# A transformer block's cross attention: scores turned so that the keys lie on the partitions, and the softmax of one sequence moved beside the projections of the next

## The reference, cut to what matters

```python
q = (layernorm(x) @ Wq) ; k = context @ Wk ; v = context @ Wv        # split in 8 heads of 64
attn = softmax(einsum('bhnd,bhmd->bhnm', q, k) * 64**-0.5, axis=-1)   # n: 128 queries, m: 2048 keys
out = einsum('bhnm,bhmd->bhnd', attn, v) ; x = x + out @ Wo + bo
```

## Time and profile before

| | |
|---|---|
| median of 3 runs | 1712.08 us (1709.21 to 1714.39) |
| the profiled execution: its time, its span | 1703.06 us, 1701.1 us |
| cross attention in it (start to the last instruction at L591) | 0 to 1140.5 us |
| busy over the span: TensorE, ScalarE, VectorE, GpSimd | 96%, 39%, 38%, 32% |
| mean granted clock of TensorE | 0.99 of 2.4 GHz |

### The profile page before, as it was taken

How to read it: one execution, slowest core, us unless ns; L and a number is a source line. 1 busy time by engine, 2 the same in 40 slices (tenths; PEclk the granted TensorE clock), 3 DMA queues, 4 the chain that set the end, 5 groups by cost and what they waited for, 6 DMA issues and landing times. The chain is left out here.

```text
span 1701.1 us, 23083 instructions
## 1 busy us (share of the span) xinstructions
PE 1634.1 (96%) x9230; PEld 1290.6 (76%) x9231; DVE 648.4 (38%) x1079; ACT 663.5 (39%) x1196; POOL 541.3 (32%) x326
## 2 busy tenths in 40 slices
PE   7999999999999999999999999998889998999998
PEld 6667887887887888788788888773457686877876
DVE  6316325424523523632532542444365461222222
ACT  3225334434433533533433443342444433354421
POOL 6221132044043023124113304003620046768661
PEclk9999999999999999999999999999999998999999
DMA  5230121121111021021012112014200076656521
GB/s 209 88 99 26 39 68 50 32 74 50 32 63 46 17 81 50 26 73 59 25 32 75 50 32 81 1 36 170 75 1 1 21 259 143 172 148 188 162 56 35
DMA packets 70393, 125.15 MB, mean 74 GB/s; under 512 B 12000, under 2 KB 28448, under 8 KB 70304
## 3 DMA queue, kind: packets, MB, share of 16 engines
q1 hardware_dynamic: 40192, 92.14, 16.6%
q10 hardware_dynamic: 25296, 23.34, 4.7%
q0 software_dynamic: 4816, 8.41, 2.6%
HBM read 100.74 MB, written 24.43 MB: 74 GB/s over the span
## 5 line engine op out<-in xcount | busy, mean ns | idle before, releaser
L220 POOL TENSOR_TENSOR ctx_h<-stage,one 128x1024 fp32r<-128x1024 f32 x62 | 117.4, 1894 | 759.1 <-PE ps_t L288 759.1
L288 PE MATMUL ps_s<-ctx_h,wk 128*128 128x512 f32 x1024 | 325.4, 393 | 9.3 <-DVE ctx_l L498 9.3
L288 PE MATMUL ps_t<-wv,ctx_h 128*128 128x512 f32 x1024 | 317.7, 392 | 0.0
L542 DVE TENSOR_TENSOR kT<-ps_s,kT 64x512 fp32r<-64x512 f32 x128 | 87.5, 683 | 426.2 <-ACT kT L455 425.4
L288 PEld LDWEIGHTS ps_s<-ctx_h,wk 128*128 128x128 f32 x1024 | 193.5, 189 | 49.7 <-issue 9.9
L288 PEld LDWEIGHTS ps_t<-wv,ctx_h 128*128 128x128 f32 x1024 | 192.3, 188 | 42.3 <-issue 2.9
L564 DVE TENSOR_REDUCE smax<-ps_s 128x1 f32<-128x1024 f32 x128 | 150.6, 1218 | 142.1 <-PE ps_s L306 140.9
L288 PE MATMUL ps_s<-ctx_l,wk 128*128 128x512 f32 x512 | 200.3, 391 | 0.0
L288 PE MATMUL ps_t<-wv,ctx_l 128*128 128x512 f32 x512 | 199.3, 389 | 0.0
L438 ACT ACTIVATE probs<-ps_s,nmax 128x1024 f32<-128x1024 f32 x128 | 142.0, 1123 | 91.6 <-DVE nmax L567 91.6
L454 ACT ACTIVATE kT<-ps_s 64x512 fp32r<-64x512 f32 x128 | 75.6, 591 | 261.8 <-PE ps_s L288 168.3
(11 more groups left out here) (236 smaller groups left out, 2228.1 us busy)
## 6 DMA issues: line engine op xcount, KB each, us to landing
stage<-in_ctx_dram SPq DMA_DIRECT2D x64, 512.0 KB, 3.8
raw_u<-in_up_dram SPq DMA_DIRECT2D x32, 512.0 KB, 4.0
stage<-in_down_dram SPq DMA_DIRECT2D x16, 512.0 KB, 4.0
raw_e<-in_down_dram SPq DMA_DIRECT2D x16, 512.0 KB, 4.1
rows_scratch<-wxo SPq DMA_DIRECT2D x25, 256.0 KB, 4.6
wxo<-rows_scratch ACTq DMA_DIRECT2D x23, 256.0 KB, 3.4
q_scratch<-kT ACTq DMA_DIRECT2D x4, 1024.0 KB, 5.5
qa<-q_scratch ACTq DMA_DIRECT2D x32, 128.0 KB, 3.0
```

The lines of the kernel that those rows point to most:

```text
L220: nc.gpsimd.tensor_tensor(hi, raw, one[:, 0:1].unsqueeze(2).broadcast_to([P, 2, QT]), ALU.mult).then_inc(hi_done, 1)
L288: mm = nc.tensor.matmul(out, w(c), m(c), start=(c + k == 0), stop=(c == DC - 1 and k == 2))
L542: nc.vector.tensor_tensor(kT[XD:P, 0, p, keys], ps_s[0:XD, p, :], kT[0:XD, 0, p, keys], ALU.subtract)
```

## The change

Scores are made with the roles exchanged: a tile of 128 keys is the weight, and the queries' hi and lo parts stand side by side in one tile `q2` as 256 columns. The result has keys on the partitions, in hi and lo halves that ScalarE copies (hi) and VectorE adds (lo) into a big tile `s`. So the probabilities need no turning. But the maximum and the sum over the keys now run across the partitions. The maximum is taken over the 16 tiles on VectorE, group by group, then turned on TensorE, reduced, put on a diagonal and spread back by a matmul with ones; VectorE subtracts it from all of `s`. The sum is made by GpSimd (`tree`) and a matmul with ones. The scores of a group are made between projections, and the softmax and `values` of `b - 1` stand in the first group of `b`. `kT` holds one group, the projections share two banks `ps_p`, and the DMAs of the queries and of the output are issued by `sp`. The value projections of groups 0 and 1 come first in sequence 0.

```diff
+            def scores(b, g, h):
+                n = nth_s(b, g, h)
+                pe.wait_ge(k_lo, 2 * (nth_k(b, g, h // 2) + 1))
+                pe.wait_ge(q_in, (b + 1) * (16 * 8))
+                if n >= 2:
+                    pe.wait_ge(s_summed, n - 1)
+                for i in range(4):
+                    mm = nc.tensor.matmul(ps_ab[:, n % 2, i].rearrange("p w t -> p (w t)"),
+                                          kT[:, h % 2, h // 2, i * P:(i + 1) * P],
+                                          q2[:, h].rearrange("p w t -> p (w t)"), start=True, stop=True)
+                mm.then_inc(s_done, 1)
...
+            for b in range(1, B):                    # TensorE
+                for p in range(PAIRS):
+                    project_k(b, 0, p)
+                    if p == 0:
+                        turn_max(b - 1, 1)
+                        turn_max(b - 1, 2)
+                    if p == 1:
+                        turn_max(b - 1, 3)
+                        spread_max(b - 1, 1)
+                    if p == 2:
+                        spread_max(b - 1, 2)
+                        spread_max(b - 1, 3)
+                for t in range(4):
+                    project_v(b, 0, t)
+                for p in range(PAIRS):
+                    values(b - 1, p)
+                keys_and_scores(b, 1)
+                values_and_scores(b, 1, lambda t: sums(b - 1) if t == 1 else None)
+                for p in range(PAIRS):
+                    project_k(b, 2, p)
+                values_and_scores(b, 2)
+                last_group(b)
...
+            def key_hi(b, g, p):                     # ScalarE
+                act.wait_ge(proj_done, projected(b, "K", g, p))
+                n = nth_s(b, g, 2 * p) - XH
+                if n >= 0:
+                    act.wait_ge(s_done, n + 2)
...
+            def copy_score(b, g, h):
+                n = nth_s(b, g, h)
+                act.wait_ge(s_done, n + 1)
+                if b and g == 0:
+                    act.wait_ge(pv_done, (b - 1) * PAIRS + h // 2 + 1)
+                    act.wait_ge(sum_done, (b - 1) * XH + h + 1)
...
+                nc.scalar.activation(s[:, h, 4 * g:4 * g + 4, :], ps_ab[:, n % 2, :, 0, :], ACT.Copy).then_inc(a_copied, 1)
+            def exps(b, h):
+                act.wait_ge(shifted, b * XH + h + 1)
+                for j in range(2):
+                    part = s[:, h, 8 * j:8 * j + 8, :]
+                    nc.scalar.activation(part, part, ACT.Exp, scale=X_SCALE).then_inc(exp_done, 1)
...
+            def add_low(b, g, h):                    # VectorE
+                nc.vector.tensor_tensor(part, part, ps_ab[:, n % 2, :, 1, :], ALU.add).then_inc(s_summed, 1)
+            def max_two(b, h):                       # reduce of 1024 elements: groups 0 and 1
+                nc.vector.tensor_reduce(pm[:, h, :], s[:, h, 0:8, :].rearrange("p c t -> p t c"), AX_X, ALU.max)
...
+            def max_group(b, g, heads, count):       # reduce of 512 elements, then the merge into pm
+                    nc.vector.tensor_reduce(pmx[:, h % 2, :], s[:, h, 4 * g:4 * g + 4, :].rearrange("p c t -> p t c"),
+                                            AX_X, ALU.max).then_inc(part_max, 1)
...
+                    nc.vector.tensor_tensor(pm[:, h, :], pm[:, h, :], pmx[:, h % 2, :], ALU.max).then_inc(count, 1)
...
+            def diagonal(b, p):
+                nc.vector.tensor_reduce(mcol[:, 2 * p:2 * p + 2], max_room(p).rearrange("p (e t) -> p e t", e=2), AX_X, ...
+                nc.vector.tensor_tensor(diag[:, p % 2], ident (broadcast), mcol (broadcast), ALU.mult).then_inc(diag_done, 1)
+            def shift(b, h):
+                largest_score = max_room(h // 2)[:, h % 2 * T:(h % 2 + 1) * T].unsqueeze(1).broadcast_to([P, MT, T])
+                nc.vector.tensor_tensor(s[:, h], s[:, h], largest_score, ALU.subtract).then_inc(shifted, 1)
+            def output(b):
+                nc.vector.reciprocal(on[:, :, :].rearrange("p h t -> p (h t)"), ps_m[:, :]).then_inc(r_done, 1)
...
+            for b in range(1, B):
+                shift(b - 1, 0)
+                key_low(b, 0, 0)
+                diagonal(b - 1, 1)
+                diagonal(b - 1, 2)
+                key_low(b, 0, 1)
+                shift(b - 1, 1)
+                diagonal(b - 1, 3)
+                key_low(b, 0, 2)
+                key_low(b, 0, 3)
+                for h in range(2, XH):
+                    shift(b - 1, h)
...
+            def tree(b, h):                          # GpSimd: 3 adds of 512 elements, one of 256, one of 128
...
+            for b in range(B):
+                for k in range(4, LB):
+                    split_ctx(b, k)
+                if b < LASTB:
+                    for k in range(4):
+                        split_ctx(b + 1, k)
+                for h in range(XH if b < LASTB else XH // 2):
+                    tree(b, h)
```

More of the change, by code:

```diff
@@ L257, in turn_x, with sums @@
+            def sums(b):
+                pe.wait_ge(sum_done, (b + 1) * XH if b < LASTB else b * XH + XH // 2)
+                if b == LASTB:
+                    pe.wait_ge(late_sum, XH // 2)
+                for h in range(XH):
+                    mm = nc.tensor.matmul(ps_m[h % 2 * XD:(h % 2 + 1) * XD, h // 2 * T:(h // 2 + 1) * T], ones[:, :],
+                                          sum_room(b, h), start=True, stop=True)
+                mm.then_inc(l_done, 1)
             def turn_x(n):
@@ L399, in _, with keys_and_scores, values_and_scores @@
-            for b in range(B):
-                batch(b, b == 0)
+            def keys_and_scores(b, g, also=None):
+                for p in range(PAIRS):
+                    project_k(b, g, p)
+                    scores(b, g - 1, 2 * p)
+                    scores(b, g - 1, 2 * p + 1)
+                    if also:
+                        also(p)
+            def values_and_scores(b, g, also=None):
+                for t in range(4):
+                    scores(b, g, 2 * t)
+                    scores(b, g, 2 * t + 1)
+                    project_v(b, g, t)
+                    if also:
+                        also(t)
@@ L489, in _ @@
+            for h in range(XH):
+                exps(LASTB, h)
         @block.vector
@@ new lines, in last_group @@
+            def last_group(b):
+                for t in range(4):
+                    for h in (2 * t, 2 * t + 1):
+                        add_low(b, NQ - 1, h)
+                    max_group(b, NQ - 1, (2 * t, 2 * t + 1), pm_done)
+                    if t == 1:
+                        diagonal(b, 0)
+            statistics(0)
+            normalise(0)
+            for n in range(HB):
+                copy_xT(n)
+            statistics(1)
+            normalise(1)
+            for n in range(2):
+                query_low(n)
@@ new lines, in _ @@
+            for p in range(PAIRS):
+                key_low(0, 0, p)
+                if p < 2:
+                    query_low(p + 2)
+                else:
+                    copy_xT(2 * p)
+                    copy_xT(2 * p + 1)
+            for p in range(PAIRS):
+                key_low(0, 1, p)
+                add_low(0, 0, 2 * p)
+                add_low(0, 0, 2 * p + 1)
+                query_low(PAIRS + p)
+            for p in range(PAIRS):
+                key_low(0, 2, p)
+                add_low(0, 1, 2 * p)
+                add_low(0, 1, 2 * p + 1)
@@ new lines, in _ @@
+            shift(LASTB, 0)
+            diagonal(LASTB, 1)
+            diagonal(LASTB, 2)
+            shift(LASTB, 1)
+            diagonal(LASTB, 3)
+            for h in range(2, XH):
+                shift(LASTB, h)
+            for h in range(XH // 2, XH):
+                dve.wait_ge(exp_done, 2 * (LASTB * XH + h + 1))
+                nc.vector.tensor_reduce(sum_room(LASTB, h), s[:, h, :, :].rearrange("p c t -> p t c"), AX_X, ALU.add) \
+                    .then_inc(late_sum, 1)
+            output(LASTB)
```

688 lines of the change are left out of this document (393 added, 295 removed).

## The result

| | before | after |
|---|---|---|
| median of four runs each | 1712.15 us (1709.21 to 1714.39) | 1774.53 us (1772.0 to 1776.1) |
| ratio | 1 | 1.0364, 95% interval 1.0344 to 1.0384 |
| span of the profiled execution | 1701.1 us | 1774.3 us |
| end of cross attention in it | 1140.5 us | 1203.3 us |
| mean granted clock | 0.99 | 0.956 |

The changed kernel is 3.6% slower, 62 us. The forecast was 1685, 1.6% faster, and its range ended at 1745, so the measured time lies 30 us beyond it. In the two profiles the end of cross attention moved by 62.8 us.

The account below looks back on a forecast made before the run. TensorE, busy 96% of the span, was taken as the bound. Opening 162.4 + 7 sequences x 130.1 (119.4 work, 9.3 waits, 1.4 clock) + tail 39.6 = 1112.7 against 1140.5, giving 1685 us; range 1640 to 1745.

Parts of the forecast that it names:

- the price of the reduces: VectorE's strided reduces for the maxima, priced as dense ones: 0.69 us for 512 elements, 1.22 for 1024.
- rival B: VectorE's reduces from SBUF are also held by GpSimd: +7 us a sequence, +49, 1734 us; chance 0.14.
- Step 2 of the waits: Second group's keys and scores: a round's chain takes 4.1 us against 3.7 of content, losing 1.2 a sequence.
- Content of TensorE: TensorE's work in one sequence without waits: 119.4 us, 13.0 less than before.
- rival D: Weight loads of the score matmuls not hidden, scores at 0.2267 us each: +103 us, 1789; chance 0.07.
- First group: TensorE waits for the diagonals on VectorE, mainly before the third spreading: 5.8 us lost a sequence.
- Rival A: Holds and gap are mild, first group loses 2.8, no clock fall: 125.1 us a sequence, 1646 us; chance 0.20.
- Group 2's values and group 3: TensorE's waits for late VectorE in later stages; the fourth group was to lose 0.7 us a sequence.
- The hold of merges beside the splits: VectorE merges with two SBUF inputs wait up to 2.4 us for GpSimd's splits, on average some 1.1.
- The trees: GpSimd's sums over the keys' tiles: 5.3 us each with four gaps, ready 2 us before the copies need them.
- rival C: Late GpSimd trees delay score copies: slower than before from 6.3 us a tree, 1722 us at 6.5; chance 0.09.
- The tail: Last sequence's softmax with nothing to hide it: 39.6 us, including four sums of 2.3 and an inverse of 4.6.

Follow-up runs that it names:

- run 1: Changed kernel with the maxima's reduces reading side-by-side elements (wrong maxima, timing only): ratio 1.0139 to the kernel before.
- run 5: Changed kernel with side-by-side reduce reads (wrong maxima) and, in group 1, each value projection ahead of its two heads' scores: ratio 0.9990 to the kernel before.
- the third edit: Diagonals one shift earlier, third spreading behind the fourth key projection, exponentials of head 1 later; alone on the changed kernel: ratio 1.0200 to the kernel before.
- run 7: Changed kernel with side-by-side reduce reads (wrong maxima), value projections ahead of scores in group 1, and diagonals one shift earlier: 1676.3 us, ratio 0.9790 to the kernel before.
- runs 2: Changed kernel with each value projection ahead of its two heads' scores in group 1 (sequence 0: group 2), reduces still strided: ratio 1.0316 to the kernel before.

## Why the prediction was wrong

**The step that failed first: the price of the reduces** ("1.22 to reduce 1024, so 1.04 ns an element", "a reduce of 512 0.69"). They measured 1.98 and 1.07, in both kinds 1.7 times. The mechanism, VectorE's work between TensorE's projections, was right, the term mis-sized. I named it at the end as what would make the forecast wrong, "twice the price would put 20 us a sequence on VectorE", and gave it no chance and no place in the range. At 1.7 times it put 12.2 there, 4.4 of which came out in the period, 38 us in all by run 1. That is near rival B's place and size (+49 forecast, 1734), by another mechanism: B was a hold by GpSimd, and no reduce was held.

**The second: a wait left out.** Step 2 of the waits has the chain right (4.1 forecast, 4.30 measured) but follows it only within the stage of keys and scores, where a projection covers 2.7 of it. At the joint of two stages nothing covers it: 3.0 of wait, and 1.6 or 2.6 of clock. `last_group` has no such joint, sequence 0 has one (3.00 at 120.2). It was to be had by writing down the order of TensorE's list across the calls, not within each. Removing it beside dense reads was worth 25 us, run 5.

Together they are 1.0369 - 0.9990, or 65 us of the 90 by which the forecast missed; the third edit took 34 more (0.9990 to 0.9790) by removing a wait that the forecast had counted. So run 5 is the one to hold against the forecast. Its cross attention ends at 1134.9, still 22 us above 1112.7: 1.3 in the opening, 2.7 in each period, 1.8 in the tail. In the period it is group 2 that is longer, 28.3 against 25.8 by the steps, with waits of 1.26 and 0.68 for VectorE: a third place where VectorE comes late, which the forecast had at nothing.

**The rest, by its own steps.**

- Content of TensorE: 3% low. With the clock at 1.00 TensorE is busy for 123.2 us a sequence (run 7), against 119.4; the busy time also holds the end of the last matmul ahead of each wait (0.39 long in a step of 0.227). 8 matmuls of scores start 0.119 apart, 0.144 behind a short wait (forecast 0.126), so rival D is out. `values` 14.2 (13.7), sums 1.0 (1.0).
- First group: 5.1 of waits at the place named (5.8), the clock's fall behind it about 1.6 (1.4), the stage 44.3 (43.8). Rival A is out.
- Group 2's values and group 3: waits of 2.96 and 1.27 for VectorE's adds (L732), where 0 and 0.7 were counted; with dense reads the first is 0.48 and the second gone (run 1).
- The hold of merges beside the splits: wrong. The forecast had four a sequence held up to 2.4 us. Their mean is 308 ns, their median 291, and of all 128 one lasted over 0.51 us (1.49). Of the diagonals two a sequence were held, 2.16 and 0.80.
- The trees: 1.31, 1.28, 1.28, 0.73 and 0.47, with gaps 5.5 (5.3 forecast), and rival C needed 6.3. It is out.
- The inverse: 3.35 us, not 4.6; the line through two small inverses overshot.
- The tail: late sums of 3.59 instead of 2.3, four of them, +5.2, less 1.2 for the inverse: 43.3 against 39.6. These sums are reduces 512 bytes apart too, the first step again.
- The queries' way: 7.7 of waiting against 5.4.
- The shifts: right (2.28 against 2.3).

What stays open is how 12.2 us more on VectorE turn into 4.3 of idle time on TensorE: runs 2 and 5 show that the two causes meet, and no run gives a rule for it.

## What to carry to other kernels

Price an operation by a row with its access pattern, not only its size; if no row has it, put both prices in the range and measure it first, as one look at a single reduce would have turned this forecast. When work is interleaved by hand, write out the merged list of the engine that bounds and look at each place where one loop ends and the next begins. To a wait of 3 us on TensorE the clock added 2.6 us, 1.6 us or nothing, so a long gap can be worth splitting or filling, even with useless work, but a single sequence does not tell its price: look at all of them. And removing one cause while VectorE stays full only moves the wait (8 us alone, 25 in company).

## What the runs showed of the hardware

- VectorE's reduce from SBUF, float32: 1.19 to 1.33 ns an element dense (679 ns for 512, 1215 for 1024), 1.93 to 2.09 at a distance of 512 bytes, 1.88 to 2.06 at 64 bytes, and the dense price in runs of four elements (1214). The Trainium skill, SBUF — State Buffer, section "Door 1: The DMA port swizzle", has a rule that fits: SBUF has lines of 16 bytes, and each access that goes on to a new line pays. The durations of all four patterns agree with it; the prediction had not drawn on it.
- The same spacing of 16 bytes: ScalarE's write of 512 elements 1111 ns in place of 597; TensorE's streamed operand of 128 float32 columns 0.114 us a matmul in place of 0.055. At 1024 bytes in PSUM, VectorE's read cost nothing (687 against 683), and GpSimd's last two steps in runs of two and one were no slower (613 and 415 ns against 733 and 467; durations on GpSimd are rough).
- The granted clock stayed at 1.00 through waits of 0.3 us. Behind the seven waits of 3.0 at the joint it was half for 3.4 us (five) or 6.8 us (two), behind those of 4.2 for 3.4 us, and behind waits of 2.95 in the values of group 2 for 6.8 us in two sequences and not at all in five.
